# Four square roots moved behind the last exponentials on ScalarE, ahead of the first silu

## The reference

```python
y = gelu(xn @ w_y + b_y);  xb = xn @ w_x + b_x
conv = conv_b + sum of conv_w[k] * xb shifted, for 4 taps
gate_x = sigmoid(conv @ w_ig + b_ig);  gate_a = sigmoid(conv @ w_ag + b_ag)
log_a = -8 * gate_a * softplus(a_param)
a = exp(log_a);  mult = sqrt(1 - exp(2 * log_a))      # first token of a sequence: a = 0, mult = 1
h = scan over tokens of a * h + gate_x * conv * mult
attn = (h * y) @ w_out + b_out
# w1q, w3q, w2q: each weight rounded to -s, 0 or +s, with s the mean of its absolute values
ffn = (silu(xn @ w1q.T) * (xn @ w3q.T)) @ w2q.T       # hidden size 682
```

## Time and profile before

| | |
|---|---|
| median of 3 runs | 78.32 us (78.19 to 381.07) |
| profiled execution, its own time | 78.11 us |
| its span, first to last instruction | 76.3 us |
| PE busy | 70.2 us, 92% |
| DVE busy | 62.0 us, 81% |
| ACT busy | 49.9 us, 65% |
| POOL busy | 31.8 us, 42% |

### The profile page before, as it was taken

How to read it: one execution, slowest core, us unless ns; L and a number is a source line. 1 busy time by engine, 2 the same in 40 slices (tenths; PEclk the granted TensorE clock), 3 DMA queues, 4 the chain that set the end, 5 groups by cost and what they waited for, 6 DMA issues and landing times.

```text
span 76.3 us, 1057 instructions
## 1 busy us (share of the span) xinstructions
PE 70.2 (92%) x364; PEld 59.4 (78%) x364; DVE 62.0 (81%) x98; ACT 49.9 (65%) x76; POOL 31.8 (42%) x42
## 2 busy tenths in 40 slices
PE   4997999989998999999999999849999999999960
PEld 4995698858885678888888789648878888899950
DVE  4694999999999999999969999789999999400340
ACT  3483716998999999999989669994347419100000
POOL 6175674049563730070008958340007818910000
PEclk9999999999999999999999999999999999999999
DMA  0999999800000000000000000000000000340062
GB/s 4 285 253 370 377 402 388 282 11 0 0 0 0 4 0 0 0 0 0 5 0 0 9 0 0 0 0 0 0 0 0 0 0 0 108 167 9 0 206 69
DMA packets 5063, 5.63 MB, mean 74 GB/s; under 512 B 493, under 2 KB 4546, under 8 KB 5058
## 3 DMA queue, kind: packets, MB, share of 16 engines
q1 hardware_dynamic: 4914, 5.55, 21.3%
q10 hardware_dynamic: 144, 0.01, 0.1%
HBM read 4.51 MB, written 1.05 MB: 73 GB/s over the span
## 4 chain that ended last, share of the span: by engine, by line
PE 42%; DVE 29%; issue 10%; ACT 8%; DMA 4%; POOL 3%; ACTq 0%; DVEq 0%
PE slot L667 12%; PE slot L650 11%; PE slot L700 9%; PE slot L711 9%; DVE conv L493 9%; DVE xn_y L450 5%; DMA x_sb<-x 4%; DVE stats L437 4%; DVE xt_lo L456 3%; DVE w_raw L515 2%; ACT ta L363 2%; ACT L332 2%; POOL g_lo L257 2%; DVE w_raw L559 2%; ACT below L408 1%
## 5 line engine op out<-in xcount | busy, mean ns | idle before, releaser
L257 POOL TENSOR_TENSOR g_lo<-w_raw,g_hi 128x512 fp32r<-128x512 f32 x10 | 14.8, 1492 | 17.9 <-ACT g_hi L338 17.9
L667 PE MATMUL slot<-xt_lo,w_q 128*128 128x512 f32 x40 | 15.7, 394 | 0.0
L667 PE MATMUL slot<-xt_hi,w_q 128*128 128x512 f32 x40 | 15.7, 393 | 0.0
L700 PE MATMUL slot<-w_q,g_hi 128*128 128x256 f32 x40 | 10.2, 293 | 1.3 <-POOL g_lo L257 1.3
L332 ACT ACTIVATE w_raw<-slot,scale 128x512 f32<-128x512 f32 x10 | 6.8, 686 | 4.9 <-PE slot L667 4.9
L700 PE MATMUL slot<-w_q,g_lo 128*128 128x256 f32 x40 | 9.8, 282 | 0.0
L493 DVE SCALAR_TENSOR_TENSOR conv<-slot,par,conv 128x511 f32<-128x511 f32 (+2 forms) x12 | 9.0, 749 | 0.4
L700 PEld LDWEIGHTS slot<-w_q,g_hi 128*128 128x128 f32 x40 | 7.6, 191 | 1.8 <-POOL g_lo L257 1.7
L667 PEld LDWEIGHTS slot<-xt_lo,w_q 128*128 128x128 f32 x40 | 7.5, 188 | 1.7
L667 PEld LDWEIGHTS slot<-xt_hi,w_q 128*128 128x128 f32 x40 | 7.5, 188 | 1.7
L338 ACT ACTIVATE g_hi<-w_raw 128x512 fp32r<-128x512 f32 x10 | 6.3, 630 | 3.2 <-DVE w_raw L515 2.9
(11 more groups left out here) (105 smaller groups left out, 144.1 us busy)
## 6 DMA issues: line engine op xcount, KB each, us to landing
w_raw<-w13t SPq DMA_DIRECT2D x2, 682.0 KB, 7.6
w_raw<-dense SPq DMA_DIRECT2D x5, 256.0 KB, 5.8
out<-x_sb SPq DMA_DIRECT2D x3, 256.0 KB, 2.2
w_raw<-w2t SPq DMA_DIRECT2D x1, 640.0 KB
x_sb<-x SPq DMA_DIRECT2D x2, 256.0 KB, 3.0
x_sb<-x SPq DMA_DIRECT2D x1, 512.0 KB, 5.4
out<-x_sb SPq DMA_DIRECT2D x2, 128.0 KB, 1.7
w_raw<-w2t SPq DMA_DIRECT2D x2, 42.0 KB
```

Source lines behind the costliest of these rows:

```text
L257: nc.gpsimd.tensor_tensor(g_lo[:, j, s], g[:, n % RING], g_hi[:, j, s].bitcast(f32), ALU.subtract).then_inc(g_lo_set, 1)
L667: mm = nc.tensor.matmul(slot[H_SLOT[s][j]][:, o], w13_q[:, c, col:col + P], v[:, s, c], start=(c == 0 and v is xt_hi), stop=(c == KC - 1 a ...
L700: mm = nc.tensor.matmul(out_tile(s, i, t), v[:, s, rows], w2_q[:, j], start=(first and j == 0 and t == tiles.start and k == 0), stop=(not ...
```

## The change

On ACT the four roots are called directly behind `decays(1)` and ahead of `silu_of(0)`. Before, the first stood behind `g_hi_of(3)` and the other three behind `g_hi_of(4)`. Nothing else is moved on any engine, and no wait of another engine is changed.

```diff
@@ -399,6 +399,9 @@
             gate_x(1)
             gate_a(1)
             decays(1)
+            for s in range(SEQS):
+                for c in range(KC):
+                    mult_of(s, c)
             act.wait_ge(w_lo_set, WIG + 1)
             silu_of(0)
             silu_of(1)
@@ -413,11 +416,7 @@
             g_hi_of(2)
             silu_of(4)
             g_hi_of(3)
-            mult_of(0, 0)
             g_hi_of(4)
-            mult_of(0, 1)
-            mult_of(1, 0)
-            mult_of(1, 1)
             for n in range(FULL, 2 * FULL):
                 silu_of(n)
                 if n > FULL:
```

## The result

The changed kernel takes 86.85 us (median of 4 runs, 85.94 to 87.02) against 78.29 us (now the median of 4 runs, one of which took 381.07): a ratio of 1.106, 95% interval 1.104 to 1.109. All ratios here leave out a run that took over 1.5% longer than the fastest of its kernel; the medians and ranges have every run. The forecast was slower, at 81.0 us with a range of 79.8 to 82.2. The direction was right and the size wrong by a factor of three: 8.6 us instead of 2.9. The profiled execution took 86.81 us, its span is 85.0 us, against 78.11 and 76.3 before. The 1.8 us around the span stayed, and so all of the loss lies in the span.

The account below looks back on a forecast made before the run. PE, busy 92% of the span, was taken as the bound, with a second half of solid matmuls. First silu 4.18 us later, less 1.25 returned, gave 2.93: 78.11 + 2.93 = 81.04 us, range 79.8 to 82.2.

Parts of the forecast that it names:

- The new place, step by step: On ACT, Sqrt load, four roots and Silu load ahead of the first silu: it starts at 42.32, 4.18 us later.
- What waits for it: On PE, hidden(3) waits for g until 43.88, 2.54 us of new idle time; down(0) could start at 47.58.
- What comes back: At block 4 of down(0), 1.25 of the 4.18 us return; hidden(5) starts at 55.03, 2.93 us later.
- all of it moves by the full 4.18: The ACT and DVE path from first silu to the g pair of n = 3, 4 shifts by 4.18 us.
- The 1.25 us that were to come back: Path time gained by removing the load and root between the high parts of n = 3 and 4: 1.25 us.
- The clock: Half clock on PE after the wait ahead of hidden(3): up to 1.7 us more, 82.7; 13% together with DVE delays.
- Is something else late behind it?: Second half: g_of(5) on DVE ends at 60.3, hidden(8) is due at 60.6, so no further delay.
- The cover of 0.3 us ahead of `hidden(8)`: Slack between the end of g_of(5) on DVE and hidden(8) on PE, shrinking from 0.7 to 0.3 us but holding.
- the rivals: Delay absorbed at PE's block 4 wait, 79.3 (10%); saved ACT load, 76.8 (2%); DVE or clock, 81.5 to 82.7 (13%).
- the forecast's own 2.93 us: Delay of block 4 of down(0) and hidden(5) on PE, carried to the end: 2.93 us; main case, 75%.

Follow-up runs that it names:

- pool_first: Changed kernel with one small memset on DVE ahead of the tail's low part, so POOL's low part of n = 3 starts first: 84.27 us.
- roots_last: Kernel before the change with its first root moved behind the high part of n = 4, where the other three stand: 78.07 us, ratio 0.997.
- fill_first: Changed kernel with 11 unused matmuls on PE ahead of hidden(2) only: 86.56 us.
- fill_down: Changed kernel with unused matmuls on PE only in down(0), 8 ahead of block 3 and 4 ahead of block 4: 84.02 us.
- fill_all: Changed kernel with unused matmuls on PE, 11 ahead of hidden(2), 14 and 4 ahead of blocks 3 and 4 of down(0): 84.28 us.
- after_lo_wait: Changed kernel with DVE's low part of the tail waiting for POOL's fifth low part: 83.09 us, ratio 1.059.
- fill_g_first: Changed kernel with DVE's g of n = 3 and 4 ahead of the tail's casts, plus unused matmuls in PE's waits: 82.0 us, ratio 1.047.

## Why the prediction was wrong

By its own steps:

- **The new place, step by step: right.** The Sqrt load waited for the first square (0.39 us), the four roots took 2.56 (forecast 2.57), each load 1.28, and the first silu came at 42.56 (forecast 42.32). That a saved load is no gain where the removed one stood in idle time was right as well.
- **What waits for it: right for the wait, not for what follows.** `hidden(3)` started at 44.15 (forecast 43.88), with 2.46 us of wait (2.54). But `down(0)` started at 49.52 instead of 47.58, with the slower clock in between.
- **What comes back: wrong.** This is the step that failed first: "all of it moves by the full 4.18". It shifted a part of the trace as a block, and kept the durations. But the engines did not shift as one. In the kernel before, the silu of n = 3 waited 0.66 us for PE and held the high part of n = 2 behind it; the rows are ACT's, DVE's cast and POOL's low part of n = 2:

```profile
43.38 0.69 ACT L332 ACTIVATE w_raw<-slot,scale 128x512 f32<-128x512 f32 x1 [0.66 <-PE slot L667]
43.97 0.62 ACT L338 ACTIVATE g_hi<-w_raw 128x512 fp32r<-128x512 f32 x1
```

```profile
44.47 0.69 DVE L568 CAST gt<-w_raw 42x1024 fp32r<-42x1024 f32 x1
```

```profile
44.67 1.65 POOL L257 TENSOR_TENSOR g_lo<-w_raw,g_hi 128x512 fp32r<-128x512 f32 x1 [0.78 <-ACT g_hi L338]
```

Behind the late first silu it did not wait, in the changed kernel:

```profile
46.46 1.25 ACT L332 ACTIVATE w_raw<-slot,scale 128x512 f32<-128x512 f32 x2
48.04 0.63 ACT L338 ACTIVATE g_hi<-w_raw 128x512 fp32r<-128x512 f32 x1 [0.32 <-DVE w_raw L514]
```

So the high part moved by 4.07 us and DVE's cast by 4.39, and POOL's low part of n = 2 came ahead of the cast instead of behind it (1.0 us). Then DVE's low part of the tail came 0.05 us ahead of POOL instead of behind it (1.0 of the 1.9 us). The rest of the 1.9 is the low part of n = 4, for which the prediction took 1.28 us. It took 2.2 in the changed kernel, in `pool_first` and in `roots_last`: once it stands directly behind that of n = 3, it meets an operation of DVE whichever engine is first. I had the row with 2.32 us for an operation that takes 1.22 alone in front of me, and took it as a duration, when it was a wait that could change sides. The 1.25 us that were to come back were not there either: `roots_last` measured 0.3.

- **The clock: undervalued.** It was a rival, with "up to 1.7 us more", laid at the wait ahead of `hidden(3)`. There it did fall, and that cost nothing (`fill_first`, `fill_down`). It fell again behind the longer waits in `down(0)`, which the forecast did not have because it missed the clashes, and cost 2.6 us there (`fill_all`; 0.5 in the one short fall of `fill_first`), in the part of the chain where PE is the bound and nothing hides it. The Trainium skill, "TensorE: Matmul & The Clock Gate", section "HAM oscillation — how this bites in real kernels", warns of this kind of loss, waits between bursts of matmuls that bring the slow clock back for the next burst; this trace agrees, with 0.50 behind waits of 1.89 and 0.99 us in a row. How much of the next burst then runs at the slow clock differed between executions of one kernel, as `fill_first` shows.
- **Is something else late behind it?** The cover of 0.3 us ahead of `hidden(8)` was thin, as said. In the changed kernel PE was so late that it never counted; where a clash was taken away or moved it was a wait of 0.30 or 0.31 us, in six kernels.
- **The range** held the rivals one at a time. The clock and the longer waits came together, since the waits are the cause of the fall; even with the clock's part taken out the kernel is at 84.3 (`fill_all`), and with the clash at the tail's low part taken out at 83.1 (`after_lo_wait`), both outside 79.8 to 82.2. No run isolates the forecast's own 2.93 us. The nearest is `fill_g_first`, 3.6 us above the kernel before (82.0 against 78.36), with a clash still on its path.

What stays open: which wait brings a fall, and how long the fall lasts. The profile of `pool_first` shows a wait of 2.45 us ahead of `hidden(3)` and a clock of 1.00 behind it, and that of the changed kernel a wait of 2.46 us with a fall to 0.50. Of the changed kernel's own four runs three took 86.81 to 87.02 with a mean granted clock of 0.94, and one 85.94 with 0.959. So the same wait may or may not bring a fall, and the runs don't say what decides.

## What to carry to other kernels

A step that moves by some microseconds moves its neighbours on other engines against each other; before shifting a piece of a trace as a block, look in it for operations that take about twice as long as their equals, since these may hold a wait for another engine's operation, and ask who is first after the shift. On a kernel that PE bounds, put whatever is not urgent on ACT behind what PE waits for, even at the price of one more table load: here ACT idled 1.86 us behind the load that was removed, and the load that was put on the path cost about its 1.28 us. Price new PE waits twice, once as a wait and once as a slower clock behind it, and ask for each fall whether PE is the bound in the stretch that follows.

## What the runs showed of the hardware that I had not expected

- A POOL and a DVE operation on SBUF that start 0.05 us apart run one behind the other, not side by side: 1.22 and 2.3 us or 2.3 and 1.3 us, by who came first. With a memset of 0.17 us ahead of one of them the whole kernel was 2.6 us faster, in its profile 0.9 us by the new order and 2.1 by a shorter fall of the clock.
- At the granted clock of 0.50 a matmul of 128x512 comes every 0.43 us instead of 0.23. Filling matmuls in the waits kept the clock at 1.00 and gave back 2.57 us without any result of use.
- Two waits on PE of nearly the same length, 2.45 and 2.46 us, went with and without a fall of the clock.
